# Attention in causal blocks: score tiles of two heads' 64 queries with 128 or 64 keys, and new orders of the work

## The reference

```python
q, k, v = dequant_matmul(x, qw_q/k/v, scales)      # 32 query heads, 8 key/value heads, 128 channels each
q, k = apply_rope(q), apply_rope(k)                # k, v shared by 4 query heads
scores = q @ k.T / sqrt(128), masked above the diagonal
ctx = softmax(scores) @ v
x = layernorm(x + dequant_matmul(ctx, qw_o, scales_o))
x = layernorm(x + cross_attention(x, ctx_4096))    # 16 heads of 32, softmax over the batch axis
x = layernorm(x + expert_lora_ffn(x))
```

## Time and profile before

| | |
|---|---|
| times of three runs | 679.2, 676.06, 680.47 us, median 679.2 |
| the profiled execution | 676.55 us, its span 674.8 us, so 1.75 us lie around the span |
| mean granted clock of TensorE | 0.992 |
| TensorE, VectorE, ScalarE, GpSimd busy | 95%, 82%, 69%, 62% of the span |
| phases 1 to 14 | 28.1 and 28.4 us in turn, from 58.9 to 454.4 us |
| before them, behind them | 58.9 us, 220.4 us |

### The profile page before, as it was taken

How to read it: one execution, slowest core, us unless ns; L and a number is a source line. 1 busy time by engine, 2 the same in 40 slices (tenths; PEclk the granted TensorE clock), 3 DMA queues, 4 the chain that set the end, 5 groups by cost and what they waited for, 6 DMA issues and landing times.

```text
span 674.8 us, 11004 instructions
## 1 busy us (share of the span) xinstructions
PE 639.5 (95%) x3294; PEld 444.9 (66%) x3294; DVE 556.5 (82%) x880; ACT 465.8 (69%) x1271; POOL 420.9 (62%) x372
## 2 busy tenths in 40 slices
PE   8989999999999999999999999998998999978996
PEld 4566787877878777787777877765565444447552
DVE  5878999998999999999899989974462968998357
ACT  6697887979779797797977979776644545622100
POOL 2478899899899989989989998881230000012003
PEclk9999999999999999999999999999999998999998
DMA  7864523533351351253234124240010000020003
GB/s 232 261 166 114 154 69 96 151 109 94 110 141 46 88 165 33 59 153 90 60 111 132 43 61 114 89 127 0 1 63 0 1 1 1 0 98 2 0 1 124
DMA packets 30187, 56.72 MB, mean 84 GB/s; under 512 B 4784, under 2 KB 5040, under 8 KB 29616
## 3 DMA queue, kind: packets, MB, share of 16 engines
q1 hardware_dynamic: 30128, 56.02, 29.4%
HBM read 32.93 MB, written 2.10 MB: 52 GB/s over the span
## 4 chain that ended last, share of the span: by engine, by line
PE 76%; DVE 9%; ACT 4%; issue 3%; POOL 3%; DMA 2%; SPq 1%; POOLq 0%; DVEq 0%; ACTq 0%
PE ps L1527 23%; PE ps L1589 18%; PE ps L1570 8%; PE ps L1542 8%; PE ps L1597 6%; PE ps L1552 4%; PE ps L1880 3%; DMA arena<-in_qkv 2%; DVE arena L1386 2%; ACT arena L993 1%; PE ps L1770 1%; DVE arena L1359 1%; DVE late L1354 1%; DVE late L1367 1%; PE ps L1871 1%
## 5 line engine op out<-in xcount | busy, mean ns | idle before, releaser
L1140 DVE SCALAR_TENSOR_TENSOR arena<-ps,arena 128x512 f32<-128x512 f32 x288 | 212.5, 745 | 15.7 <-PE ps L1527 3.8
L1527 PE MATMUL ps<-x_hi,w_sb 128*128 128x512 f32 x384 | 170.9, 445 | 5.1 <-ACT arena L790 2.2
L1527 PE MATMUL ps<-x_lo,w_sb 128*128 128x512 f32 x384 | 150.8, 393 | 0.0
L1168 DVE SCALAR_TENSOR_TENSOR y<-ps,arena,y 128x512 f32<-128x512 f32 x192 | 138.2, 744 | 12.6 <-PE ps L1589 8.5
L799 ACT ACTIVATE arena<-ps,small 128x128 f32<-128x128 f32 x256 | 90.7, 378 | 31.3 <-DVE small L1146 26.8
L624 POOL TENSOR_TENSOR arena<-arena,consts 128x512 f32<-128x512 f32 x75 | 96.9, 1291 | 22.7 <-DVE arena L1140 22.7
L1589 PE MATMUL ps<-heads_hi,wo_sb 128*128 128x512 f32 x256 | 108.7, 425 | 0.1
L630 POOL TENSOR_TENSOR arena<-arena,consts 128x512 f32<-128x512 f32 x75 | 96.8, 1290 | 12.6 <-DMA arena<-arena 10.4
L749 POOL TENSOR_SCALAR var_eps<-mean_var 128x2 f32<-128x2 f32 (+1 forms) x13 | 7.3, 561 | 154.4 <-DVE mean_var L1278 154.4
L1589 PE MATMUL ps<-heads_lo,wo_sb 128*128 128x512 f32 x256 | 101.0, 395 | 0.0
L640 POOL TENSOR_TENSOR arena<-arena 128x512 f32<-128x512 f32 x75 | 96.6, 1287 | 5.6
(11 more groups left out here) (146 smaller groups left out, 967.6 us busy)
## 6 DMA issues: line engine op xcount, KB each, us to landing
arena<-arena SPq DMA_DIRECT2D x160, 128.0 KB, 2.3
arena<-in_qkv SPq DMA_DIRECT2D x48, 256.0 KB, 3.9
arena<-in_o SPq DMA_DIRECT2D x32, 256.0 KB, 3.7
...
```

The costliest lines, as they stand in the source:

```text
L1140: nc.vector.scalar_tensor_tensor(acc, group_bank(p, KC * c + g), scale_of(p // 2, c, g), acc, ALU.mult, ALU.add).then_inc(dve_scaled, 1)
L1168: nc.vector.scalar_tensor_tensor(dst, by_tile(out_bank(p, u)), out_scale_of(p // 2, u), dst, ALU.mult, ALU.add).then_inc(out_added, 1)
L1527: mm = nc.tensor.matmul(group_bank(p, u), w_sb[:, c, g, :], part[:, g, half * HALF:(half + 1) * HALF], start=(k == 0), stop=(k == 1))
```

## The change

**Causal blocks.** A tile of scores was 128 queries x 128 keys of one head, half of it masked. Now the 128 queries of a tile are taken in halves, and `q_t` is laid out so that the same 64 queries of two heads stand side by side. Per tile there are two matmuls of two heads' later 64 queries with all 128 keys, and two of two heads' earlier 64 queries with their 64 keys: 384 columns of scores instead of 512 (`SC = 384`). In every odd tile the two halves of the tokens are exchanged in the input (`x_t`) and in the rotation tables, so that its early keys lie on partitions 64 to 127. `probs_low` then puts the short parts of an even and an odd tile side by side, and one transpose turns both.

**Turning and weighing.** `turn_probs` makes two transposes for an even tile and four for an odd one (two of these are of the short parts of both). `weigh_v` works on a pair of tiles: two matmuls of 256 columns over all 128 rows, into banks 6 and 5, and two of 256 columns over 64 rows, the even tile's on partitions 0 to 63, the odd one's on 64 to 127. Bank 5 is still the bank of the transposes, so TURNS has two more entries.

**Other engines.** Row maxima in two reduces a tile; exponentials and scaling of two parts with 128 and two with 64 columns; mask and copies shorter. `rotate` writes the query tiles in eight pieces of 64 columns. Conversion of tiles 3, 4 and 5 goes from GpSimd to ScalarE. `scales` and `out_scales` become tensors of their own. The orders of all engines are written anew, and PRODUCTS with them.

```diff
+POOL_WEIGHTS = [0, 1, 2]
+ACT_WEIGHTS = [3, 4, 5]
...
 PRODUCTS = (
-    "G0 G1 G2 O0 G3 G4 G5 G6 O1 G7 G8 G9 G10 G11 O2 O3 O4 O5 G12 O6 O7 O8 G13 G14 G15 O9 G16 G17 G18 G19 G20 "
-    "G21 O10 O11 G22 G23 O12 O13 O14 O15").split()
+    "G0 G1 G2 G3 G4 G5 G6 G7 G8 O0 G9 O1 G10 G11 G12 G13 O2 O3 G14 G15 G16 O4 O5 G17 O6 G18 G19 O7 G20 O8 G21 "
+    "O9 G22 G23 O10 O11 O12 O13 O14 O15").split()
...
-TURNS = "V T0 T1 T2 T3".split()
+TURNS = "V T0 T1 W0 T2 T3 W1".split()
...
+        def score_part(i):
+
+            return slice(P * i, P * i + P) if i < 2 else slice(2 * P + LOW * (i - 2), 2 * P + LOW * (i - 1))
...
+        def probs_low(n, i):
+
+            return probs[:, n // 2 % 2, 4 * P + P * (i - 2):4 * P + P * (i - 1)]
...
+        def q_out(h, half):
+
+            return q_blocks[:, half * BPH:(half + 1) * BPH, :, h // 2, h % 2, :]
...
-                dst = (k_t if c == 0 else q_t[:, c - 2, :])[:, half * HALF:(half + 1) * HALF]
-                nc.gpsimd.tensor_tensor(dst, raw_cos[:, i % 2, :], turned[:, i % 2, :], ALU.add).then_inc(rotated, 1)
+                dst = by_block(k_t[:, half * HALF:(half + 1) * HALF]) if c == 0 else q_out(c - 2, half)
+                nc.gpsimd.tensor_tensor(dst, by_block(raw_cos[:, i % 2, :]), by_block(turned[:, i % 2, :]),
+                                        ALU.add).then_inc(rotated, 1)
...
+            def convert(j, c):
+
+                wait(act, w_in, 16 * NT * j)
+                wait(act, group_done, GROUPS * (2 * j - 1) + KC * (c + 1))
+                nc.scalar.activation(w_sb[:, c], w_int[:, c], ACT.Copy, bias=-ZERO).then_inc(act_w_ready, 1)
...
-                nc.vector.tensor_reduce(neg_max[:, s, :], score_ps[s][:, :].rearrange("p (h k) -> p h k", k=P),
+                nc.vector.tensor_reduce(neg_max[:, s, 0:2], bank[:, 0:2 * P].rearrange("p (h k) -> p h k", k=P),
+                                        AX.X, ALU.max, negate=True)
+                nc.vector.tensor_reduce(neg_max[:, s, 2:4], bank[:, 2 * P:SC].rearrange("p (h k) -> p h k", k=LOW),
                                         AX.X, ALU.max, negate=True).then_inc(max_done, 1)
...
-                for h in range(QPK):
-                    mm = nc.tensor.matmul(score_ps[s][:, h * P:(h + 1) * P], q_t[:, h, b * P:(b + 1) * P],
-                                          k_t[:, b * P:(b + 1) * P], start=False, stop=(n >= 2 or h == QPK - 1),
+                for i in range(QPK):
+                    low = i >= 2
+                    queries = q_blocks[:, b, b % 2 if low else 1 - b % 2, i % 2].rearrange("p m q -> p (m q)")
+                    keys = k_t[:, low_tokens(b) if low else slice(b * P, (b + 1) * P)]
+                    mm = nc.tensor.matmul(bank[:, score_part(i)], queries, keys, start=False, stop=(n >= 2 or i == QPK - 1),
                                           skip_group_check=(n >= 2))
...
-                for h in range(QPK):
-                    mm = nc.tensor.transpose(turn_ps[:, h * P:(h + 1) * P], probs[:, s, h, :], ident)
+                for i in range(2):
+                    mm = nc.tensor.transpose(turn_ps[:, i * P:(i + 1) * P], probs_part(n, i), ident)
+                if n % 2:
+                    for i in range(2, 4):
+                        mm = nc.tensor.transpose(turn_ps[:, i * P:(i + 1) * P], probs_low(n, i), ident)
...
-                nc.tensor.matmul(pv_ps[:, :], v_sb[:, b, :], probs_t[:, s, :, :].rearrange("p h q -> p (h q)"),
-                                 start=True, stop=True).then_inc(pv_done, 1)
+                for i in range(2):
+                    nc.tensor.matmul(pv_ps[i][:, 2 * P:4 * P], v_sb[:, n % NB + i, :], probs_t[:, 2 * P * i:2 * P * (i + 1)],
+                                     start=True, stop=True)
+                for i in range(2):
+                    rows = slice(LOW * i, LOW * (i + 1))
+                    mm = nc.tensor.matmul(pv_ps[i][:, 0:2 * P], v_sb[rows, n % NB + i, :], probs_t[rows, 4 * P:6 * P],
+                                          start=True, stop=True)
+                mm.then_inc(pv_done, 1)
```

436 lines of the change are left out of this document (238 added, 198 removed).

## The result

The changed kernel takes 675.4 us (median of 20 runs, 673.67 to 677.67), the one before 678.5 us beside it (20 runs, 675.43 to 680.47): ratio 0.9957, interval 0.9944 to 0.997. It is 3 us faster, where 15 us were forecast. The profiled execution took 674.36 us, 2.2 us less than that of before. Two runs are slow ones and left out of all figures: one of a_all, of 1246 us, and one of the kernel before, of 1082 us, beside the pads.

The account below looks back on a forecast made before the run. TensorE was taken as the bound, savings up to some 2 us a phase coming through. Steady phases 12.9 us, phase 0 1.4 and phase 15 0.7 sum to 15.0 us: 679.2 - 15 = 664 us, range 650 to 682.

Parts of the forecast that it names:

- the margin of 2 us: Steady phases: VectorE 2.0 us and GpSimd 1.7 to 3.1 us behind TensorE, so savings up to some 2 us come through.
- What bounds the kernel: Head phases 1 to 14: TensorE is the bound, 27.6 us of work and 0.65 us of stall a phase.
- Transposes: TensorE, pair of tiles: six transposes instead of eight at 0.11 us each, saving 0.44 us a phase, all on the path.
- Scores: TensorE, scores of a tile: streaming 64 instead of 128 columns in two of four matmuls saves 0.
- The rival of half the cost: TensorE scores: 64-column matmuls cost half, 0.89 us a phase saved; 28 us faster in all, 651 us; chance 0.12.
- Weighing V: TensorE, pair of tiles: halves overlap, shape changes cost 0.19 us; 1.48 us against 1.72, saving 0.48 us a phase.
- The other engines: A phase: VectorE +0.15 us, ScalarE -0.8, GpSimd -0.93, all hidden while TensorE's 26.7 us stands above.
- The new order: Steady phases: stalls as large as the 0.65 us of before, elsewhere; phase 27.3 us, 14 x 0.92 = 12.9 us saved.
- The walk: One phase by row prices: GpSimd is the narrow place, period at least 26.2 us plus waits of 0.4.
- Rival one: No change: halves don't overlap, or GpSimd's waits stay as before; 1 to 7 us faster, 672 to 678 us; chance 0.24.
- Both ends: Phase 0 gains 1.4 us on GpSimd's chain, phase 15 gains 0.7 us, the tail is not touched.
- Rival three: GpSimd: rotation sums writing 64-column pieces take 0.4 us more each; 10 us slower, 689 us; chance 0.14.

Follow-up runs that it names:

- a_all: Changed kernel with tile 2's full-row weighing earlier, last rotation sum without sine, all four tiles' cuts over one column: 670.1 us, ratio 0.9875 to the kernel before.
- the pads: Changed kernel and kernel before, each with one more unread 256-column matmul a phase on TensorE: 681.3 us (ratio 1.0027) and 683.2 us (1.0058).
- b_pad: Kernel before with one more unread 256-column matmul on TensorE ahead of the fourth tile's weighing in each phase: 683.2 us, ratio 1.0058.
- b_less: Kernel before, old order, from phase 2 on three transposes instead of four a tile and weighings over 448 of 512 columns: 674.3 us, ratio 0.9939.
- a_dve2: Changed kernel with one more unread VectorE maximum over the heads of tile 1, ahead of that tile's cut: 684.5 us, ratio 1.0091 to the kernel before.
- a_cut: Changed kernel with VectorE reading output product O14 ahead of the cut of tile 2's heads: 675.5 us, ratio 0.9967 to the kernel before.
- a_early: Changed kernel with the full-row weighing of tile 2 two products earlier on TensorE: 673.2 us, ratio 0.9927 to the kernel before.

## Why the prediction was wrong

Two steps failed, and they cost about the same: the margin of 2 us up to which savings on TensorE were to come through, and the size of the saving on the weighings.

**What bounds the kernel.** "TensorE is the bound ... no saving beyond some 2 us a phase can come through". TensorE was on the path: 0.44 us added to it cost 0.41 us a phase in the kernel before (b_pad). What failed is the margin, read from busy sums (VectorE 2.0 us, GpSimd 1.7 to 3.1 us behind). b_less measures it: of 0.88 us a phase taken off TensorE in the old order, 0.13 come through in the steady phases, 0.3 by the whole times. A TensorE that is busy all the time in a window, and a chain of waits with nothing but its work in it, showed that it was hardly ever late, not that the others were early. The 2 us by which VectorE's busy time lay lower were no slack, since VectorE spends them waiting at fixed places and comes back late.

**Transposes.** Right: two take 0.14 us (245.38 to 245.52) and 0.08 us more before the product behind them is at its pace, 0.22 us; six are 0.66 us a pair, and 0.44 us a phase of work is saved. How much of it comes through is the question above.

**Scores.** Right: eight passes, four of them with 64 columns, take 0.82 us (229.08 to 229.90) and 0.08 us behind them, 0.9 as before. The rival of half the cost is out: with fp32 weights of 128 columns, 64 streamed columns take what 128 do. By the Trainium skill (TensorEngine Tiling (Array Packing), Performance Considerations), where the fixed part of a matmul is worth some 60 columns, they should have taken clearly less; the measurement decides.

**Weighing V.** Right in kind, since the two halves overlap: four passes of 256 columns in 0.64 us, where one after the other they need 0.86. Mis-sized in the price of the change of shape: a pair costs 1.69 us and not 1.48, so the saving is 0.03 us a pair and not 0.24, 0.06 us a phase and not 0.48. By columns a pair is 0.86 + 0.43 = 1.29 us. The change of shape therefore costs 0.40 us and not 0.19: 0.09 on the full-row passes ahead, 0.21 on the halves, 0.10 on the product behind. The loads fit this: they don't run ahead into or out of the half shape, 0.33 us idle each way. With it agrees what the Trainium skill says (TensorEngine Tiling (Array Packing), Tiling Modes), that the engine drains at such a change. The forecast's price came from L1935 and L1941, whose passes also differ in length and in weights; that they hid a part of it is a guess.

**The other engines.** ScalarE's and GpSimd's busy time in the windows from 87 to 426 us fell by 0.8 and 0.9 us a phase, as forecast. VectorE's was to grow by 0.15, because the sum took the durations of overlapping neighbours; from start to start the two reduces of a tile take 0.53 us (256.44 to 256.97), the one before took 0.59 (256.88 to 257.47), so its work fell a little. Two things were seen rightly: GpSimd's last sum had no margin left, and VectorE's cut of tile 1 ends 0.2 us before the third turn (a_dve2 shows what that is worth). But they were called hidden, on the ground of their busy sums.

**The new order.** "I expect stalls as large as the 0.65 us of before": they are 1.1 us. By stretches of the profiled executions 12.8 us were missed (15.0 forecast, 2.2 found): 11.2 in the thirteen steady phases (5.5 by the weighings, 5.7 by stalls, in which savings are waited for again), 2.5 in the step into the last phase, 1.3 in phase 0, and -2.3 in the last phase with the tail. The walk found the scores' wait for GpSimd, which stands in four phases of fourteen. It left out the bank of O14 behind VectorE's stop of 0.87 us, a stop that comes with the pairing. Taking that wait away alone gives nothing, though (a_cut), and shortening the piece behind which VectorE stands gives 0.15 us a phase (a_early). Rival one had this time (672 to 678 us) and this saving (0.06 us a phase), from halves that don't overlap or from GpSimd's waits. The halves do overlap, so that its number fits is luck for the first; the second is in the trace and worth 1 to 2 us.

**Both ends.** Phase 0's 1.4 us did not come: its first two conversions begin at 36.32 us instead of 35.75 (they wait for their DMA), and the first sine behind them at 37.72 instead of 37.37 us. Behind it GpSimd waits 0.60 us for a sum of VectorE and 0.21 us for a copy, so its last sum ends at 57.30 us, 0.3 us earlier than before. The step into the last phase costs 1.6 us more: TensorE's first keys wait 1.45 us for ScalarE's late reading of O15, which nobody forecast. The last phase gives 3.0 us with the tail instead of 0.7, of which up to 1.8 us are the granted clock and not the change. In it waits of 2.15 and 0.88 us of TensorE for ScalarE's copies are gone, and new ones of 1.6 us for VectorE and 0.8 us for ScalarE stand there.

**Rival three** (slower rotation sums) is refuted: they take 1.29 us as before. Its remark on pieces of 128 columns is not in the earlier trace rows; the trace has it for L648, 1290 ns on average.
